# A rebuilt opening stage in a fused adaLN block: on-chip B u and first state, smaller pieces, weights awaited one by one

## What is computed

```python
def _L0_attn_ref(x, ln_w, ln_b, W_in, conv_w, A, Bm, Cm, W_out):
    h = layernorm(x) * ln_w + ln_b
    proj = h @ W_in
    data, gate = (proj[..., :INNER], proj[..., INNER:])       # INNER = 384
    xp = jnp.pad(data, ((0, 0), (K - 1, 0), (0, 0)))          # K = 3
    conv = sum((xp[:, j:j + seq, :] * conv_w[:, j] for j in range(K)))
    u = jax.nn.silu(conv)
    M = jnp.eye(S, dtype=x.dtype) + A.T                       # S = 16
    Bu = jnp.einsum('bti,si->tbs', u, Bm)
    def step(state, bu_t):
        s = state @ M + bu_t
        return (s, s)
    _, states = jax.lax.scan(step, init, Bu)                  # over all tokens
    y = jnp.einsum('tbs,is->bti', states, Cm)
    out = jax.nn.sigmoid(gate) * y @ W_out
    return x + out

mod = (_silu(c) @ wmod).reshape(1, 6, 1, -1)                  # sa, ca, ga, sb, cb, gb
h = _layernorm(x) * (1 + ca) + sa
x = x + ga * _L0_attn_ref(h, ...)
h = _layernorm(x) * (1 + cb) + sb
x = x + gb * _L0_ffn_ref(h, ...)
```

## Time and profile before

| what | value |
|---|---|
| time, median of 3 runs | 1452.16 us (1449.67 to 1452.58) |
| the profiled execution, its own time | 1451.81 us |
| its span in the trace | 1450.1 us |
| mean granted TensorE clock over the span | 0.978 |
| PE busy / DVE / ACT / POOL | 95% / 80% / 46% / 49% of the span |
| first scan step begins, scan ends | 60.60, 73.00 us |
| first h2 complete | 97.97 us |
| first DVE accumulation of slot (0, 0) | 119.61 us |

### The profile page before, as it was taken

The page is one execution under the profiler, slowest core; times in us unless marked ns, Lnnn a source line. Parts: engine busy times, 40 slices in busy tenths (PEclk is TensorE's granted clock), DMA queues, the critical chain, the costliest instruction groups (busy, mean ns, idle before and its releaser), DMA issues. The chain is left out here.

```text
span 1450.1 us, 20840 instructions
## 1 busy us (share of the span) xinstructions
PE 1375.9 (95%) x6884; PEld 1208.9 (83%) x6884; DVE 1157.6 (80%) x2192; ACT 672.9 (46%) x1331; POOL 709.5 (49%) x628
## 2 busy tenths in 40 slices
PE   5578999999999999999999999999999999999998
PEld 3458989999999999999999966878787887878776
DVE  5758587686875868767677888999999999989876
ACT  3340221302213013131011089888888888888983
POOL 3222131311312213112014167888888888989897
PEclk8688999999999999999999999999999999999999
DMA  4230110011110111010116450010000000000000
...
DMA packets 84668, 63.24 MB, mean 44 GB/s; under 512 B 15520, under 2 KB 77392, under 8 KB 84304
## 3 DMA queue, kind: packets, MB, share of 16 engines
...
...
## 5 line engine op out<-in xcount | busy, mean ns | idle before, releaser
L1474 PE MATMUL ps<-w_hi,memory_r 128*128 128x384 f32 x2048 | 569.2, 343 | 5.7 <-DVE w_lo L887 2.7
L1247 DVE SCALAR_TENSOR_TENSOR wst<-ps,w_cur,wst 128x384 f32<-128x384 f32 x480 | 295.3, 615 | 169.7 <-PE ps L1474 156.3
L1474 PEld LDWEIGHTS ps<-w_hi,memory_r 128*128 128x128 f32 x2048 | 376.2, 189 | 9.9 <-DVE w_lo L887 2.9
L1691 POOL TENSOR_TENSOR memory_rest<-memory_rest,pf 128x512 f32<-128x512 f32 x248 | 346.3, 1396 | 66.9 <-ACT pf L1798 58.3
L1474 PE MATMUL ps<-w_lo,memory_r 128*128 128x384 f32 x1024 | 344.6, 337 | 0.0
L1864 DVE TENSOR_TENSOR p_lo<-pf,p_hi 128x512 fp32r<-128x512 f32 x256 | 282.4, 1103 | 34.2 <-ACT p_hi L1800 33.2
L1474 PEld LDWEIGHTS ps<-w_lo,memory_r 128*128 128x128 f32 x1024 | 194.0, 189 | 4.7 <-issue 1.4
L1798 ACT ACTIVATE pf<-ps 128x512 f32<-128x512 f32 x256 | 153.1, 598 | 71.5 <-PE ps L1970 55.7
L1758 ACT COPY ps<-shift_rows 128x512 f32<-128x512 f32 x254 | 151.7, 597 | 5.9
L1800 ACT ACTIVATE p_hi<-ps 128x512 fp32r<-128x512 f32 x256 | 152.1, 594 | 0.0
L1845 DVE TENSOR_REDUCE mx<-ps 128x1 f32<-128x512 f32 x224 | 147.6, 678 | 1.2 <-PE ps L1959 1.2
...
## 6 DMA issues: line engine op xcount, KB each, us to landing
...
v_scratch<-wst ACTq DMA_DIRECT2D x60, 64.0 KB, 1.8
...
```

Of the source, the lines that this page charges most:

```text
L1247: nc.vector.scalar_tensor_tensor(out=dst, in0=src, scalar=w, in1=dst, op0=ALU.mult, op1=ALU.add).then_inc(moe_acc, 1)
L1474: ins = nc.tensor.matmul(ps[:, s % MOE_BANKS, 0:H3], x_part[p][:, k, rows], w_part[:, k, e].rearrange("p t h -> p (t h)"), start=(k == 0 a ...
L1691: nc.gpsimd.tensor_tensor(p_sum[:, p], p_sum[:, p], pf[:, j % PB], ALU.add).then_inc(p_summed, 1)
```

## The change

It touches the opening and what slot (0, 0) needs of it; blocks from (1, 0) on run the same operations as before, block (0, 1) apart from its B u.

- **Powers.** The 16 small DMAs that wrote A and A^T on the diagonal become two that repeat A down the partitions (`a_rep`); DVE multiplies them by a mask (`own_group`, made by POOL). Powers 1 and 2 are squared before the projection and copied by DVE, 3 to 5 between the data projections and 6 to 8 after scan steps 0 to 2, copied by ACT.
- **Modulation.** The first third of the product is split: first scale, then shift, each 256 columns and with a semaphore of its own.
- **Conv and u** of block (0, 0) go group by group: evacuation, two DVE operations, ACT's sigmoid, DVE's product.
- **B u** of blocks (0, 0) and (0, 1): `first_input_term`, 24 matmuls of 64 columns with shifted windows of a zero-padded `b_wide` (it lies in w_all's memory) put B u in the 128x64 layout directly into PSUM; DVE copies it (`take_input`). For (0, 1) they stand behind step 3 of slot (0, 0), and the copy to w_all that is part of the route moves to step 9.
- **First states**: `spread_states`, 8 matmuls with 16 columns of the identity each, and two copies on ACT, one subtraction on DVE, in place of `states_round(0, 0)`.
- **Output and second norm** of block (0, 0) go tile by tile: `first_x2`, `first_h2`, POOL's root, ACT's square.
- **Weights**: `W_STAGE` lets experts 0 to 5 take three staging buffers in turn and 6 to 15 two (before: 0 to 11 three, 12 to 15 two). ACT's and DVE's `split_w` calls stand at other places. PE waits for w_lo expert by expert in the first tile of slot (0, 0), not for all 16 before it.
- **Order**: PE's projection of block (0, 1) stands behind the output of block (0, 0); the low parts 0 to 8 stood ahead of the conv of block (0, 1) on DVE, and now only 0 to 5 do.

The diff, cut to its core:

```diff
+        BU_LATE, W_ALL_LATE, SHIFT_BANK = 3, 9, 3
...
-        W_STAGE = [e % 3 if e < E - 4 else e % 2 for e in range(E)]
+        WIN_LO, SIM_SQ, COL_SS, CM_LO, WOUT, SIM_N = 1, 2, 3, 4, 5, 6
+        THIRDS = 6
+        W_STAGE = [e % 3 if e < THIRDS else e % 2 for e in range(E)]
...
-            return 3 if isinstance(i, int) and 2 * i + p == 0 else 0
+            return 4 if is_first(i, p) else 0
...
+                load_mod(0)
+                sp.dma_start(win, w_in.rearrange("(k p) n -> p k n", p=P)).then_inc(win_in, 16)
+                for l, src in enumerate((a_mat_t, a_mat)):
+                    sp.dma_start(a_rep[:, l], src.rearrange("(a s) j -> a s j", a=1).to_broadcast([NB, S, S])
+                                 ).then_inc(a_in, 16)
...
-                load_w(0, 6)
+                load_w(0, 3)
...
+                load_w(3, 4)
                 x_load(0, 1)
-                scan_load(0, 0)
-                load_w(6, 9)
-                states_round(0, 0)
-                load_w(9, E)
+                load_w(4, E)
                 x2_store(0, 0)
-                scan_load(0, 1)
...
+                link_b.block(0, 0)
...
+                row_norms(0, 0)
                 conv_out(0, 1)
-                second_norm(0, 0)
-                row_norms(0, 0)
                 residual(0, 1)
...
                 hidden(0, 0)
...
+                split_w(0, 1)
...
+                for f in range(FI):
+                    evacuate_projection(f, f + 1, 0, 0)
+                    pow_copy(3 + f)
+                act.wait_ge(ht_lo_ready, 1)
+                for f in range(FI):
+                    act.wait_ge(conv_ready, f + 1)
...
+                split_w(1, 2)
+                for k in range(3 + FI, SCAN):
+                    pow_copy(k)
+                split_w(2, 4)
...
                 hidden(0, 1)
-                split_w(6, 9)
+                split_w(4, 5)
                 data_out(0, 1)
-                split_w(9, 12)
-                conv_sigmoid(0, 1)
-                gates_out(0, 1)
-                split_w(12, 14)
-                bu_store(0, 1)
-                act.wait_ge(w_lo_ready, E - 4)
+                split_w(5, 7)
+                act.wait_ge(w_lo_ready, THIRDS)
                 row_squares(0, 0)
                 x_parts(0, 0)
-                split_w(14, E)
+                gates_out(0, 1)
+                split_w(7, 9)
+                conv_sigmoid(0, 1)
+                split_w(9, E)
                 exp(0, 0)
...
+                    dve.wait_ge(out_mm, t + 1)
+                    dve.wait_ge(r_ready, 1)
+                    tt(x2[:, t], x2[:, t], ps[:, OUT_BANKS0[t], 0:C], ALU.add
+                       ).then_inc(x2_ready, 1)
+                    dve.wait_ge(x2_ready, t + 1)
+                    op(nc.vector.bn_stats(bst[:, 2, t], x2[:, t]))
+                    more.wait()
+                    nc.vector.bn_aggr(mv[:, 2, t], bst[:, 2, t]).then_inc(mv2_ready, 1)
+                    dve.wait_ge(mv2_ready, t + 1)
+                    op(modulate(h2, x2, 2, 4, t, t + 1))
+
+                def first_h2(t):
+
+                    dve.wait_ge(dve_b, 2 * t + 2)
+                    dve.wait_ge(rs2_ready, t + 1)
+                    shift(h2, 2, 3, t, t + 1).then_inc(h2_ready, 1)
...
+                dve.wait_ge(a_in, 32)
+                dve.wait_ge(pool_const, OWN_GROUP)
+                blocks = [powers[:, 0, pad:], powers_t[:, 0]]
+                for l, blk in enumerate(blocks):
+                    ins = tt(blk.rearrange("p (g s) -> p g s", s=S),
+                             a_rep[:, l:l + 1].to_broadcast([P, NB, S]), own_group, ALU.mult)
+                pre.done(ins)
...
+                first_conv(0)
...
+                first_conv(1)
+                split_w(0, 1)
+                first_conv(2)
+                for f in range(FI):
+                    dve.wait_ge(csig_ready, f + 1)
+                    tt(sg[:, f], sg[:, f], cv[:, f], ALU.mult).then_inc(u_ready, 1)
+                norm_piece(0, 0, 1)
...
+                take_input(0, 0, BU_BANK0)
+                dve.wait_ge(r_ready, 1)
+                dve.wait_ge(mv_ready, 3)
...
+                ins.then_inc(dve_const, 1)
+                scan_step(8, 0, 0)
+                norm_piece(4, 0, 1)
+                dve.wait_ge(st_hi_ready, 1)
+                low = slice(CM_ROW, CM_ROW + S)
+                tt(st_parts[low, :], ps[0:S, ST_BANK0, :], st_parts[0:S, :].bitcast(F32), ALU.subtract
+                   ).then_inc(s_parts_ready, 1)
+                split_w(2, 3)
                 gate_times_y(0, 0)
+                split_w(3, 4)
+                more.block(0, 0)
...
+                split_w(4, 6)
                 for n in range(TAPS - 1):
                     conv_piece(n, 0, 1)
-                split_w(9, 12)
-                for n in range(X2_PIECES):
-                    x2_piece(n, 0, 0)
-                split_w(12, E)
-                for n in range(ROUTE_PIECES):
+                split_w(6, E)
+                for n in range(ROUTE_PIECES - 1):
                     route_piece(n, 0, 0)
 
...
+                pe.wait_ge(wmod_in[0], 16)
+                for bank, cols in ((X0, slice(C, 2 * C)), (SHIFT_BANK, slice(0, C))):
+                    for k in range(KC):
+                        ins = nc.tensor.matmul(ps[:, bank, cols], c_bc[:, k, :], wmod_ld[:, k, cols],
+                                               start=(k == 0), stop=(k == KC - 1))
...
+                    if f == 0:
+                        pe.wait_ge(late_in, 16 * N_LATE)
+                    pe.wait_ge(u_ready, 1 + f if not p else 1 + FI)
+                    for g in range(NB):
+                        ins = nc.tensor.matmul(ps[:, bank, 0:GT], b_wide[:, B_AT[f] - S * g:B_AT[f] - S * g + P],
+                                               sg[:, f, g * GT:(g + 1) * GT],
+                                               start=(f == 0 and g == 0), stop=(f == FI - 1 and g == NB - 1))
...
+                def spread_states():
+
+                    pe.wait_ge(scan_add, SCAN)
+                    for g in range(NB):
+                        ins = nc.tensor.matmul(ps[0:S, ST_BANK0, g * GT:(g + 1) * GT], ident[:, g * S:(g + 1) * S],
+                                               scan_s[SCAN % 2][:], start=True, stop=True)
...
+                for f in range(FI):
+                    project(f, 0, 0)
+                    next_power(3 + f)
+                for f in range(FI, 2 * FI):
+                    project(f, 0, 0)
+                for f in range(FI):
+                    first_input_term(f, 0, 0, BU_BANK0)
+                column_norms()
+
+                for k in range(SCAN):
+                    pe.wait_ge(pow_ready, k + 1)
+                    scan_piece(k, 0, 0, first=True)
+                    if 3 + FI + k < SCAN:
+                        next_power(3 + FI + k)
+                spread_states()
+                pe.wait_ge(dve_const, CM_LO)
+                pe.wait_ge(dve_const, WOUT)
+                pe.wait_ge(proj_evac, 2 * FI)
+                y_piece(0, 0, 2)
+                n2_transposes(0, 1)
+                out_piece(0, 0)
...
                 for f in range(2 * FI):
-                    project(f, 0, 0)
-                    next_power(2 + f)
-                column_norms()
-                input_term(0, 0)
-
-                pe.wait_ge(bu_ready, 1)
-                n2_transposes(0, 1)
-                pe.wait_ge(col_ss, 1)
-                next_power(8)
-                pe.wait_ge(pow_ready, SCAN)
-                for k in range(SCAN):
-                    scan_piece(k, 0, 0, first=True)
-                for f in range(FI):
-                    project(f, 0, 1, early=True)
-                pe.wait_ge(parts_ready, 1)
-                pe.wait_ge(wout_ready, 1)
-                pe.wait_ge(proj_evac, 3 * FI)
-                y_piece(0, 0, 2)
-                out_piece(0, 0)
-                for f in range(FI, 2 * FI):
-                    project(f, 0, 1, early=True)
-                input_term(0, 1, first=True)
-                pe.wait_ge(bu_ready, 2)
+                    project(f, 0, 1)
                 h2_transposes(0, 0)
-                pe.wait_ge(sn_ready, 1)
+                pe.wait_ge(dve_const, SIM_N)
                 logits_piece(0, 0)
-                pe.wait_ge(w_lo_ready, E)
...
+                        if is_first(i, p) and t == 0:
+                            pe.wait_ge(w_lo_ready, e + 1)
...
+                        if is_first(i, p) and s == BU_LATE:
+                            pe.wait_ge(proj_evac, 4 * FI)
+                            for f in range(FI):
+                                first_input_term(f, *c, X1)
```

438 lines of the change are left out of this document (259 added, 179 removed).

## The result

The changed kernel takes 1454.73 us in the median of 20 runs (1451.99 to 1460.77), the kernel before 1452.58 in 20 (1449.67 to 1455.04): a ratio of 1.0017, with a 95% interval of 1.0009 to 1.0025. That is 2.15 us more, where 1.0 to 1.8 was forecast (1453.6, against this 1452.58 or against the profiled 1451.81; the median at the time was 1452.16). The profiled execution has a span of 1452.1, 2.0 more than before's 1450.1.

The account below looks back on a forecast made before the run. PE's matmuls set the pace from slot (0, 0) on, so only the start of its accumulations moves the time: 1451.81 + 0.9 (later first accumulation) + 0.9 (colder clock) = 1453.6 us, range 1446 to 1460.

Parts of the forecast that it names:

- Stage A: Opening up to u of block (0, 0): u complete at 38.2 us instead of 47.90, a lead of 9.7.
- Stage B: B u on chip: first scan step at 45.5 us, bounds 43.5 and 47.5, a lead of 15.1.
- Stage C: Scan with three squarings between its steps, +1.2 us against 12.4 before: scan ends at 59.1.
- Stage D: States and y, from scan's end to gate: 4.9 us instead of 9.35, gate at 64.0, lead 18.3.
- Stage E: Output and second norm, from gate to h2: 15.4 us instead of 15.62, h2 at 79.4, lead 18.5.
- Stage F: From h2 to first accumulation: late low parts take the whole lead; first accumulation at 120.5 us, 0.9 later than before.
- the stop by h2's low part: After h2, POOL's low part of h2 (2.36 us) stops DVE's work, +2.2 us.
- The four rounds: Low parts of experts 8 to 15: two buffers, two experts a round at 5.1 us, 20.5 in all.
- rival 3: Queued loads, 3.94 instead of 3.23 us in each of four rounds, and cold clock: 1457.5 (1455.5 to 1460), chance 0.33.
- Slot (0, 0): First slot: 48 more B u records for block (0, 1) cost nothing; PE's longer idle costs clock, +0.9 us.
- Rival 1: POOL's stops fall in DVE's load waits, so the lead arrives whole after h2: 1448 us (1447 to 1449), chance 0.19.
- Rival 2: Loads run ahead, rounds are hidden and the lead comes through: 1433 us, or some 1442; chance 0.06.

Follow-up runs that it names:

- u_early: Changed kernel with DVE's u of conv groups 0 and 1 each moved ahead of the next piece; 1455.87 us, ratio 1.0024 against the kernel before.
- store_early: Changed kernel with the store of block (0, 0)'s x2 ahead of the loads of experts 10 to 15; 1455.08 us, ratio 1.0022 against the kernel before.
- noload: Changed kernel without the weight loads of experts 8 to 15, so its output is not the block's; ratio 0.9945 against the kernel before.
- thirds12: Changed kernel with three staging buffers for experts 0 to 11 again, some ACT and POOL pieces moved; 1451.43 us, ratio 0.9995 against the kernel before.
- res_late: Changed kernel with POOL's residual of block (0, 1) held until the first accumulation of slot (0, 0); 1455.4 us, ratio 1.0023 against the kernel before.
- before_late4: Kernel before with only late() = 3 made 4, its pieces one step later in slot (0, 0); 1454.0 us, ratio 1.0013 against the kernel before.
- late3: Changed kernel with late() = 4 put back to 3 in slot (0, 0); 1454.6 us in 12 runs, ratio 1.0018 against the kernel before.

## Why the prediction was right, and where it was not

The time came out 0.2% up, inside "within 0.2%" and inside the range. The reasoning was right in its main step, that the queue of weight pieces eats the lead. It was wrong in two others that happened to cancel: the opening came out 3.1 us shorter than forecast (117.36, not 120.5), and slot (0, 0) 2.8 longer than before.

- **Stage A** (u at 38.2): 37.65. One of its sums doesn't hold, "3 x 1.8 behind 23.9, at about 31", which gives 29.3; the projections ended at 30.70, since the first took 2.89 and two squarings stand behind each.
- **Stage B** (first scan step 45.5, 43.5 to 47.5): 43.69 here, 43.0 to 49.0 over the eleven profiles with this opening. The bounds from cold and full clock (4.3 to 11.3 for the 48 records) held: B u took 5.5 to 5.8 in seven of the eleven and 8.25 to 10.47 in four. I took one value for what is two. That this term makes the changed kernel's runs spread over 8.8 us is only in part so: its two values lie at most 5.0 apart, before's runs spread over 5.4, and u_early's profile has the quick B u in a run of 1456.64. Over all 20 runs the time goes with the mean granted clock: 1451.99 to 1455.20 us in the twelve runs at 0.976 to 0.980, 1455.23 to 1460.77 in the eight at 0.972 or 0.973. Where in those eight the clock was lost isn't shown.
- **Stage C** (13.6): 56.46 - 43.69 = 12.8. **Stage D** (4.9): 5.2. The sum has 0.91 for a low part and next to nothing for y; y took 1.62 and the low part lay beside it. The 16 records of the spread took 1.89 at a granted clock of 0.50, 0.118 each, half of the 0.235 that the scan's take at that clock. The narrow load that the Trainium skill speaks of in "TensorE: Matmul & The Clock Gate", section "LDWEIGHTS (loading the stationary operand)", agrees in its direction. The nearest row beside it is B u in store_early, with results as long (64 columns), 128 columns loaded and the same clock of 0.50: 10.47 / 48 = 0.218 a record.
- **Stage E** (15.4, though its terms add up to 15.7): 13.65, the term of the opening that I mis-sized most. A tile took 1.95 and not 2.15, and statistics and aggregation ran while POOL held the port; only the modulate of tile 0 was stopped (2.00 at 66.85, 0.51 for the other tiles), beside POOL's low part of the normed input (66.21 to 68.57). That is the rule of "SBUF — State Buffer", section "Who interferes with whom", in the Trainium skill: the instruction with two inputs in SBUF was stopped, the one-input ones weren't. No addition of stage E fell beside that operation of POOL, so nothing is shown for those.
- **Stage F** (h2 to first accumulation 41.1): 117.36 - 75.29 = 42.1. Its mechanism, low parts behind the second norm and rounds of two buffers, was the answer to where 20 us go: noload puts the loads' share at 10.3 us, and thirds12 shows that a third buffer shortens it. In its parts: the stop by h2's low part was 2.2, as said, only on low part 6. The four rounds from 85.04 to 109.73 took 24.7, not 20.5 + 2.3: the first two lasted 6.2 without their stop, the last two 5.0 and 5.1. In the first, two experts' loads were queued on SP, as in rival 3 (3.90 from the first issue at 85.63 to the cast at 89.53). In the second, expert 11's loads stood alone, and the third of them took 1.69 to issue instead of 0.47, at 94.37; why isn't shown. The residual's first half, which I let stop the chain, stopped the other one (res_late).
- **Together** the first accumulation came at 117.36 and not 120.5.
- **Slot (0, 0)**: this step failed. "48 more records ... cost nothing" was true. The colder start was there: 1.05 us of clock more than before by the windows, where I had put 0.9; but before's PE had a wait of 0.90 at 122.49 that is gone, so it cost next to nothing. What failed is that the diff has late() = 3 becoming 4 and the sum gives it no price. That step moves the transposes of block (1, 0) one step later while DVE's q/k low part stays at its step, with ACT's queue between them. PE's waits behind DVE near 150 and 185 grew by it from 1.94 to 4.73, in before_late4 to 4.74; the slot grew by 2.84 and 3.7, and by 1.95 between late3 and the changed kernel. In the time it is less sure: ratio 1.0013 in before_late4, nothing in late3. The question not asked was which of two pieces, one moved and one not, share an in-order queue.
- **Rivals.** Rival 1's condition (stops miss the chain) held for the residual and not for h2's low part or for u. Rival 2 (the lead comes through) was refused by the buffers, as argued: noload shows that it would have come. Rival 3's queued loads were there in one of four rounds, and a second was as long for another reason.

The forecast of almost no change was therefore earned as to the opening, and lucky by some 3 us as to the sum: 2.25 us of lead and a slot 2.84 us longer, with 1.4 of chance between two profiles. How much of the 2.15 in the medians is each can't be said closer than before_late4's 0.13% and the spread of B u.
